# Mean embedding projection: when TensorE adds its columns of the second tile, and when that tile's gathers start

## The reference

```python
valid = sequence_ids < 12500                      # 1024 users x 200 ids
safe_ids = where(valid, sequence_ids, 0)
seq_emb = emb_table[safe_ids] * valid             # 12500 x 512 table, float32
denom = maximum(valid.sum(axis=1), 1)
user_repr = seq_emb.sum(axis=1) / denom           # mean of the valid rows
logits = user_repr @ proj_w + proj_b              # 512 x 12500, float32
```

## Time and profile before

| | us |
|---|---|
| median of 3 runs | 652.95 |
| lowest, highest | 652.92, 653.26 |
| span of the profiled execution, first to last instruction | 667.9 |
| TensorE busy in that span | 616.0 |
| VectorE busy | 407.4 |
| GpSimd busy | 231.4 |
| mean granted TensorE clock | 0.985 |

### The profile page before, as it was taken

One profiled execution on the slowest core, in us unless ns is written; L12 is line 12 of the kernel. 1 busy time (PEld: TensorE's weight loads), 2 busy tenths in 40 slices (PEclk: granted clock), 3 DMA queues, 4 the chain that ended last, 5 costly groups with the idle time before them and its releaser, 6 DMA issues.

```text
span 667.9 us, 7583 instructions
## 1 busy us (share of the span) xinstructions
PE 616.0 (92%) x2602; PEld 478.9 (72%) x2602; DVE 407.4 (61%) x722; ACT 138.2 (21%) x154; POOL 231.4 (35%) x227
## 2 busy tenths in 40 slices
PE   1888499979969999999999999999999999999998
PEld 1326256747747878778788788888888888888886
DVE  7967836986967878789787545333333333334352
ACT  7606332314114113130020022011111111121210
POOL 6775856775765565666545000000000000000000
PEclk9989889998999999999999999999999999999999
DMA  9995996996978978889788259655445555656743
GB/s 312 388 357 159 380 328 213 299 379 188 326 257 276 311 249 266 284 254 340 239 252 299 93 148 298 217 169 173 147 134 176 175 178 177 210 176 185 241 128 102
DMA packets 77704, 158.31 MB, mean 237 GB/s; under 512 B 9288, under 2 KB 65043, under 8 KB 77659
## 3 DMA queue, kind: packets, MB, share of 16 engines
q1 hardware_dynamic: 60378, 110.30, 48.9%
q0 software_dynamic: 17280, 47.47, 22.7%
HBM read 115.70 MB, written 51.20 MB: 250 GB/s over the span
## 4 chain that ended last, share of the span: by engine, by line
PE 71%; DVE 15%; issue 8%; DMA 2%; another core or an unknown queue 2%; ACT 1%; DVEq 1%; POOL 0%; POOLq 0%
PE acc L792 66%; DVE sums L538 6%; PE turned L748 2%; DVE w_lo L588 2%; DMA rows<-in_L_rec_emb_table_dram,index 2%; DVE key L495 1%; DVE w_lo L586 1%; DVE top L491 1%; DVE mean L575 1%; PE turned L740 1%; ACT w_hi L414 1%; PE acc L797 1%; PE turned L723 0%; DVEq L251 0%
## 5 line engine op out<-in xcount | busy, mean ns | idle before, releaser
L343 POOL DMA_INDIRECT rows<-in_L_rec_emb_table_dram,index x208 | 221.2, 1063 | 113.1 <-issue 83.9
L792 PE MATMUL acc<-w_hi,mean_hi 128*128 128x500 f32 x800 | 225.4, 404 | 4.2 <-issue 3.3
L600 DVE TENSOR_TENSOR stage<-acc,bias_sb 128x500 f32<-128x500 f32 x162 | 109.2, 676 | 192.6 <-PE acc L792 172.7
L792 PE MATMUL acc<-w_hi,mean_lo 128*128 128x500 f32 x800 | 215.3, 391 | 2.2 <-DVE mean_lo L580 2.2
L792 PE MATMUL acc<-w_lo,mean_hi 128*128 128x500 f32 x800 | 215.4, 390 | 0.3 <-issue 0.2
L792 PEld LDWEIGHTS acc<-w_hi,mean_hi 128*128 128x128 f32 x800 | 150.5, 190 | 37.4 <-issue 9.5
L792 PEld LDWEIGHTS acc<-w_hi,mean_lo 128*128 128x128 f32 x800 | 150.9, 189 | 34.4 <-DVE mean_lo L580 2.6
L792 PEld LDWEIGHTS acc<-w_lo,mean_hi 128*128 128x128 f32 x800 | 150.6, 188 | 32.7 <-issue 1.4
L538 DVE SCALAR_TENSOR_TENSOR sums<-rows,mask,sums 128x512 f32<-128x512 f32 x165 | 123.9, 751 | 8.2
L414 ACT ACTIVATE w_hi<-w_raw 128x2000 fp32r<-128x2000 f32 x39 | 72.8, 1875 | 226.9 <-PE acc L792 209.1
L586 DVE TENSOR_TENSOR w_lo<-w_raw,w_hi 128x1000 fp32r<-128x1000 f32 x39 | 46.5, 1193 | 18.9 <-ACT w_hi L414 11.0
(11 more groups left out here) (104 smaller groups left out, 180.9 us busy)
## 6 DMA issues: line engine op xcount, KB each, us to landing
out_dram<-stage SPq DMA_DIRECT2D x200, 250.0 KB
w_raw<-in_L_rec_proj_w_dram SPq DMA_DIRECT2D x39, 1000.0 KB
bias_sb<-in_L_rec_proj_b_dram SPq DMA_DIRECT2D x39, 250.0 KB
raw_at_hi<-in_L_rec_proj_w_dram SPq DMA_DIRECT2D x4, 1000.0 KB
rows<-in_L_rec_emb_table_dram,index POOLq DMA_INDIRECT x208
raw_at_lo<-in_L_rec_proj_w_dram SPq DMA_DIRECT2D x3, 1000.0 KB
stage<-in_L_rec_proj_w_dram SPq DMA_DIRECT2D x1, 1000.0 KB
ids_sb<-in_r_sequence_ids_dram SPq DMA_DIRECT2D x1, 700.0 KB, 4.3
```

The source lines that it names most:

```text
L343: return pool.indirect_dma_start(out=dst, out_offset=None, in_=table, in_offset=bass.IndirectOffsetOnAxis(ap=column, axis=0), bounds_check ...
L600: dve.tensor_tensor(stage[:, g % STAGE, r - stores[g][0]], acc[:, r % BANKS, 0:BW], bias_sb[:, i % BIAS], ALU.add).then_inc(s_moved_by_dve, 1)
L792: last = nc.tensor.matmul(bank, first, second, start=part + k == 0, stop=part == 2 and k == K - 1 and not by_act[r])
```

## The change

TensorE's columns of a tile are all due at `joined[t] - 2`. For tile 1 that is unit 8 for all eight columns, and with them `sum_rest(1)`; their diagonals all stand at unit 7 of ScalarE's loop. For tile 2 nothing moves (both columns were due at unit 20 already). The wait of GpSimd for the first mean before column 30 is gone.

```diff
-    GATHER_LEAD, PAUSE_AT = 5, 4
+    GATHER_LEAD = 5
 
     def column_due(c):
 
         t, j = divmod(c, FAST)
         if by_pe[c]:
-            return joined[t] - 2 - (FAST - 1 - j) // 3
+            return joined[t] - 2
         begin, end = joined[t - 1] - 2 if t > 1 else 0, joined[t] - SUM_AHEAD
         return begin + (end - begin) * j // (dve_last[t] - FAST * t)
...
                         else:
                             wait_used(pool, c - ROWS + CH - 1)
-                        if c == FAST + PAUSE_AT:
-                            pool.wait_ge(s_mean_lo, 1)
                         if t > 1 and column_due(c) > GATHER_LEAD:
```

## The result

The changed kernel takes 644.42 us (median of 4 runs, 643.52 to 644.56) against 653.11 (652.92 to 654.4): ratio 0.9855, 95% interval 0.9843 to 0.9867 (the two medians alone give 0.9867). So it is faster by 1.3 to 1.6%, clear of the spread of the runs. Forecast were 643.8 and the range 641 to 649.5. All lines of the changed file behind the removed wait have numbers two lower.

The account below looks back on a forecast made before the run. TensorE was taken to bound the kernel, with a dent ahead of unit 8. Unit 8 starting at 89.4 instead of 98.60 gains 9.2 us, taken whole: 652.95 - 9.2 = 643.8 us, range 641 to 649.5.

Parts of the forecast that it names:

- What bounds the kernel: TensorE is full after the early slices; its deepest later dent, 66.8 to 83.5 us, delays everything that follows.
- Units under the wait: TensorE before tile 1's columns: units 6 and 7 move ahead, 2 x 2.94 us, reaching `sum_rest(1)` at 78.55.
- The ring and the landing: GpSimd's last tile 1 gathers: ring holds column 51 to 81.7, it lands at 87.7, unit 8 starts 89.4: 9.2 us.
- the one column at the low clock: TensorE's last column before unit 8, taken at 1.70 us instead of 0.91 because TensorE has been waiting.
- the rival of the low clock: Tile 1's eight columns run at 1.2 GHz, 1.70 us each: only 4.4 us gained, 648.6; chance 7 in 100.
- The bound from TensorE: Without any wait TensorE would reach unit 8 at 87.3, so this place gives at most 11.3 us.
- Diagonals: ScalarE's eight in unit 7, 0.40 us each, hide behind columns of 0.91; uncovered, up to 1.6 us in all.
- The joins behind: Joins of tiles 2 and 3: all moves earlier with unit 8, TensorE's waits of 1.58 and 2.62 us left unchanged.
- The rival "more": Column 51 lands in time and TensorE runs through to unit 8: 11.3 us gained, 641.7; chance 12 in 100.

Follow-up runs that it names:

- e0: The kernel before, profiled again without any edit; 652.9 us (one run).
- e10: The changed kernel itself, unedited, run again on the same chip for comparison; 644.93 us.
- e2: Against the kernel before: only GpSimd's wait for the first mean removed, columns still spread over units 6, 7 and 8; 646.74 us, ratio 0.9898.
- e9: Against e5: VectorE makes `mean_lo` of tile 1 behind column 53, ahead of the sorting step and column 54; 643.96 us.
- e4: Against the changed kernel: tile 1's first four diagonals made one unit earlier on ScalarE, ahead of block 10's split; 643.95 us.
- e5: Against e4: loads of weight blocks 11 to 14 also held back until unit 7 has been moved out; 644.83 us.
- e7: Against the changed kernel: tile 1's columns one unit ahead of the join, loads of blocks 11 to 14 held until unit 7 is moved out; 643.49 us.

## Why the prediction held

*What bounds the kernel* held: the dent is where the 9.28 us came from, and everything behind unit 8 moved as a block (e0 against the changed kernel).

*Units under the wait* held: units 6 and 7 ended at 77.97, forecast 78.55, and `sum_rest` found its rows.

*The ring and the landing* gave the right start of unit 8 by errors that cancel, which is luck. Column 50 was issued at 80.53 (forecast 80.4), but the ring held it for 0.16 us only: GpSimd itself came late, by issues of up to 1.94 us that the sum had at 1.00. Column 51 went out at 82.81 (81.7, since the issue before it took 1.97 us) and landed at 88.5 (87.7), after 5.7 us (6.02). Unit 8 started at 89.15 (89.4) none the less, since the one column at the low clock was a term too many in this execution: the clock was 1.00 throughout. In e10, of the same kernel, the rival of the low clock did come, for some of the columns, and unit 8 started only 0.4 us later, not the 4.8 that lie between the forecast's 9.2 us and the rival's 4.4. For it stood the Trainium skill's "TensorE: Matmul & The Clock Gate" (HAM oscillation), that bursts between waits for DMA start at the low clock: e0 and e2 show just that (two columns in 4.21 and 3.78 us after idle times of 6.63 and 4.25). In the changed kernel the two profiles differ: after waits of 2.21 and 0.88 us the rows show no fall, and in e10 the burst behind 2.50 us starts at the upper level and falls within it.

*The bound from TensorE* was too low at 11.3 us: a column costs 0.86 us from start to start, not 0.91, `sum_rest` at the full clock 0.86 in e9 (from 77.79 to the first column at 78.65), not 1.42, and in e9 unit 8 starts at 85.65, 12.8 us ahead of e0.

*Diagonals* were costed at nothing behind the columns. That step was wrong in its reason: they stand behind `w_high(10)`, which waits for a load, and TensorE waited 2.21 us for the first. That it cost little is the landing's doing: in e4, without that wait, TensorE waits for gathers instead and unit 8 again follows the landing of column 51. e4's time is 0.5 us lower, which is within the spread of the changed kernel's two sets of runs (644.42 and 644.93).

*The joins behind* held, but with less room than I gave them. The waits of 1.58 and 2.62 us at the joins of tiles 2 and 3 came from the first profile with its extra waits; e0 has 1.26 and 0.33, the changed kernel 1.65 and 0.36. VectorE's columns and GpSimd's gathers of tile 2 had no room left beyond about 1 us, as e5 to e9 show. The rival "more" (641.7) does not come even with an earlier unit 8: e5 and e9 start it at 87.16 and 85.65 and take 644.83 and 643.96 us.

Whether e7 beats the changed kernel is open: 0.9 us apart, with ranges that overlap and in different sets of runs.

## What to carry to other kernels

A wait that an engine must do anyway is best placed behind all the work that doesn't depend on it, and the transfers it waits for belong into the nearest stretch where the DMA is half idle; here each alone gave 5 and 6.7 us, together 8.7. Before a further step in the same place, compare where the next join lands: when its start no longer moves with the one before, another queue (here, by the traces, GpSimd's issue of gathers) has become the bound. A step that is moved on one engine should be checked for what now stands ahead of it on every engine that feeds it, here a load behind ScalarE's split.

## What was not expected of the hardware

The issue of a gather on GpSimd mostly takes 1.00 us, but 1.88 to 1.97 in five places of the changed kernel between 48 and 126 us, and 1.53 in one. Each of these overlaps a `w_lo` subtraction of VectorE, which reads two tiles from SBUF (that of block 10 from 80.44 for column 50):

```profile
80.44 1.19 DVE L584 TENSOR_TENSOR w_lo<-w_raw,w_hi 128x1000 fp32r<-128x1000 f32 x1
```

The Trainium skill's "GPSIMD Engine Reference" (Key points) says that GpSimd shares its interfaces to SBUF with VectorE, in contention with instructions that have two SBUF inputs. The trace agrees as far as the overlap goes, but not every gather beside a `w_lo` is slow (in e4 column 50's issue at 80.47 took 0.99 us and column 51's at 81.77 took 1.08, beside block 10's subtraction from 80.77), and no run here took VectorE's work away to test it.
